# A gated-memory attention layer on TensorE: one head's plain fp32 products regrouped

## What is computed

```python
def chunk_loss(ws, k, lrc, v):
    pred = _mem_mlp(ws, k)                       # silu(k @ w0) @ w1
    return jnp.sum(jnp.mean((pred - v) ** 2, axis=-1) * lrc)
grads = jax.vmap(jax.grad(chunk_loss), ...)(mem_ws, keys, lr, values)   # per chunk of 64 tokens
momentum = _assoc_scan(gm, -grads)
updates = _assoc_scan(gd, momentum)
w0 = mem_w0 + updates[0]
w1 = mem_w1 + updates[1]
x = jnp.einsum('bhncd,bhnde->bhnce', q, w0)
vals = jnp.einsum('bhncd,bhnde->bhnce', jax.nn.silu(x), w1)
vals = _rmsnorm(vals) * (mh_gamma + 1.0) * gate
out = vals @ w_combine
```

## Time and profile before

| | |
|---|---|
| median of three executions | 1114.12 us |
| the profiled execution | 1113.32 us |
| its span, first to last instruction | 1110.8 us |
| granted TensorE clock, mean | 0.987 |
| PE, PEld busy | 96%, 81% of the span |
| DVE, ACT, POOL busy | 62%, 61%, 51% |

### The profile page before, as it was taken

One profiled execution on the slowest core, in us unless ns is written; L12 is line 12 of the kernel. 1 busy time (PEld: TensorE's weight loads), 2 busy tenths in 40 slices (PEclk: granted clock), 3 DMA queues, 4 the chain that ended last, 5 costly groups with the idle time before them and its releaser, 6 DMA issues. The chain is left out here.

```text
span 1110.8 us, 19052 instructions
## 1 busy us (share of the span) xinstructions
PE 1071.7 (96%) x6613; PEld 900.1 (81%) x6613; DVE 686.0 (62%) x1752; ACT 678.7 (61%) x1356; POOL 562.4 (51%) x574
## 2 busy tenths in 40 slices
PE   6899799999999999999999999999999999999994
PEld 4666588888888888888888888888888888888883
DVE  5887566767766555565556555565556555657774
ACT  5776466677655656565556555665566565656663
POOL 6885244478874444344434444444434443444553
PEclk9999699999999999999999999999999999999997
DMA  7210300000030000000000000000000000012221
GB/s 205 79 46 29 105 1 1 1 15 30 21 97 12 19 10 9 8 21 10 9 8 11 20 11 8 9 20 11 8 8 11 20 8 6 6 42 61 69 70 42
DMA packets 42129, 32.66 MB, mean 29 GB/s; under 512 B 4042, under 2 KB 36652, under 8 KB 41900
## 3 DMA queue, kind: packets, MB, share of 16 engines
q1 hardware_dynamic: 38484, 25.93, 8.0%
q0 software_dynamic: 2304, 4.74, 1.3%
q10 hardware_dynamic: 1248, 0.79, 0.2%
HBM read 18.30 MB, written 13.41 MB: 29 GB/s over the span
## 5 line engine op out<-in xcount | busy, mean ns | idle before, releaser
L1040 DVE TENSOR_TENSOR p_sb<-bank,coef 128x512 f32<-128x512 f32 (+3 forms) x512 | 218.8, 483 | 3.1 <-PE bank L749 2.6
L1232 POOL TENSOR_TENSOR sq_rest<-sq,sq_high 128x450 f32<-128x450 f32 x64 | 67.2, 1050 | 245.1 <-ACT sq_high L934 245.1
L772 PE MATMUL bank<-p_sb,err_t 128*128 128x450 f32 (+3 forms) x512 | 132.9, 402 | 0.2 <-DVE p_sb L1040 0.2
L772 PE MATMUL bank<-p_sb,du_t 128*128 128x450 f32 (+3 forms) x512 | 128.8, 394 | 0.0
L772 PEld LDWEIGHTS bank<-p_sb,err_t 128*128 128x128 f32 x512 | 83.7, 190 | 45.5 <-DVE p_sb L1040 25.2
L1236 POOL TENSOR_TENSOR sq_low<-sq_rest,sq_mid 128x450 bf16<-128x450 f32 x64 | 67.6, 1056 | 96.5 <-ACT sq_mid L948 96.2
L772 PEld LDWEIGHTS bank<-p_sb,du_t 128*128 128x128 f32 x512 | 82.1, 190 | 41.4 <-issue 23.9
L1093 DVE SCALAR_TENSOR_TENSOR acc<-bank,rg,acc 128x128 f32<-128x128 f32 x224 | 62.9, 343 | 68.2 <-POOL rg L1220 68.2
L1118 DVE SCALAR_TENSOR_TENSOR du<-q_sb,bank 128x512 f32<-128x512 f32 x64 | 44.0, 688 | 87.7 <-PE bank L749 87.7
L1216 POOL TENSOR_TENSOR rs<-ms,neg_half 128x4 f32<-128x4 f32 x64 | 80.6, 1259 | 28.6 <-DVE ms L1075 27.3
L1207 POOL TENSOR_TENSOR s_low<-s_sb,s_high 128x512 fp32r<-128x512 f32 x64 | 82.7, 1293 | 20.2 <-ACT s_high L911 20.1
(11 more groups left out here) (297 smaller groups left out, 3103.1 us busy)
## 6 DMA issues: line engine op xcount, KB each, us to landing
sorted_rows<-coef SPq DMA_DIRECT2D x5, 516.0 KB, 5.0
rows<-sorted_rows SPq DMA_DIRECT2D x40, 64.5 KB, 1.8
x<-in_L_attn_inputs SPq DMA_DIRECT2D x8, 256.0 KB, 5.5
x_rows<-x SPq DMA_DIRECT2D x8, 256.0 KB, 2.3
ew<-in_L_ffn_w SPq DMA_DIRECT2D x8, 256.0 KB, 3.9
attn_out<-acc SPq DMA_DIRECT2D x7, 256.0 KB, 2.1
ew<-attn_out SPq DMA_DIRECT2D x7, 256.0 KB
ew<-ffn_rows SPq DMA_DIRECT2D x8, 192.0 KB
```

The costliest lines, as they stand in the source:

```text
L772: last = pe.matmul(out[:, P * i:QW], rows[:, i, :], p_sb[:, P_COL[i]:P_COL[i] + QW - P * i], start=False, stop=True, skip_group_check=True)
L1040: last = nc.vector.tensor_tensor(dst, src, w, ALU.mult)
L1232: nc.gpsimd.tensor_tensor(sq_rest[:], sq[:], sq_3[0][:], ALU.subtract).then_inc(g_rest, 1)
```

## The change

On TensorE a step gets a new order. w_x goes right behind the other three projections. The scores are split: `scores_near` (tiles 0 and 1, fp32r) and `scores_far` (tiles 3 and 2, plain). Of s the near ones stay where they were, the far ones go behind VB's product and the block's transpose (which now uses QA), right ahead of the first apply. Of f the far ones go behind the transposes of err (which now use EB), ahead of the error's product; the near ones come behind it. The output rows go ahead of the second apply. The semaphores' counts follow: far tiles count once together, near tiles one by one. VectorE weighs in the new order, and ScalarE copies err_t ahead of the square of vals. The diff, cut to its core:

```diff
-SC_ORDER = [0, 1, 3, 2]
+NEAR, FAR = [0, 1], [3, 2]
@@ TensorE, step
                         project(QA, m.w_qk, f, SHIFT).then_inc(p_qa, 1)
+                        pe.wait_ge(a_xs, n)
+                        project(XB, m.w_x, f, SHIFT)
                     if s is not None:
                         k = n_of(s)
                         pe.wait_ge(v_xl, k + 1)
                         pe.wait_ge(v_p0, SC_BANKS * (k + 1))
-                        scores(s_2[s[1] % 2], xs_2, s_sb[s[1] % 2][:, 2 * P:], xs, p_s1)
-                    if x is not None:
-                        r = s[1] % RING
-                        pe.wait_ge(m.s_rows[r], 16 * (turn(s) + 1))
-                        pe.wait_ge(a_xs, k + 1)
-                        pe.transpose(XB[:, 0:P], m.rows[r][:, 0:D], m.ident[:]).then_inc(p_t, 1)
+                        scores_near(s_2[s[1] % 2], xs_2, p_s1)
                     if f is not None:
                         pe.wait_ge(g_sl, n + 1)
...
                         product(EB[:], [w[:] for w in w1], [part[:] for part in s_2[h % 2]], start=False).then_inc(p_e, 1)
                     if s is not None:
                         pe.wait_ge(v_acc, k)
+                        product(VB[:, 0:QW], [w[:] for w in w1], [part[:] for part in xs_2])
+                    if x is not None:
+                        r = s[1] % RING
+                        pe.wait_ge(m.s_rows[r], 16 * (turn(s) + 1))
+                        pe.wait_ge(a_qa, n + 1)
+                        pe.transpose(QA[:, 0:P], m.rows[r][:, 0:D], m.ident[:]).then_inc(p_t, 1)
+                    if s is not None:
+                        pe.wait_ge(v_p1, SC_BANKS * k + 2)
+                        scores_far(s_sb[s[1] % 2][:, 2 * P:], xs, p_s1)
                         pe.wait_ge(a_et, k + 1)
-                        product(VB[:, 0:QW], [w[:] for w in w1], [part[:] for part in xs_2])
-                        apply(VB, err_t, v_p1, k).then_inc(p_v, 1)
+                        apply(VB, err_t, NEAR)
+                        pe.wait_ge(v_p1, SC_BANKS * k + 3)
+                        apply(VB, err_t, FAR).then_inc(p_v, 1)
...
                     if f is not None:
                         pe.wait_ge(a_err, n + 1)
-                        pe.wait_ge(a_xs, n)
                         for t in range(T):
-                            last = pe.transpose(XB[:, t * P:t * P + P], err[:, t * P:t * P + P], m.ident[:])
+                            last = pe.transpose(EB[:, t * P:t * P + P], err[:, t * P:t * P + P], m.ident[:])
                         last.then_inc(p_et, 1)
+                        pe.wait_ge(a_qa, n + 1)
+                        routing(s)
+                        scores_far(yw, qa, p_s0)
                         pe.wait_ge(v_el, n + 1)
                         pe.wait_ge(v_q, n + 1)
                         product(U[:], [w[:, 3, :] for w in m.w4t], [part[:] for part in err_2]).then_inc(p_d, 1)
                         pe.wait_ge(g_ql, n + 1)
-                        pe.wait_ge(v_p1, SC_BANKS * n)
-                        routing(s)
-                        scores(yk, qa_2, yw, qa, p_s0, SC_ORDER[:-1])
+                        pe.wait_ge(v_p0, SC_BANKS * n + 1)
+                        scores_near(yk, qa_2, p_s0)
                         pe.wait_ge(v_du, n + 1)
+                        pe.wait_ge(a_et, n + 1)
                         for t in range(T):
                             last = pe.transpose(EB[:, t * P:t * P + P], du[:, t * P:t * P + P], m.ident[:])
                         last.then_inc(p_dt, 1)
-                        scores(yk, qa_2, yw, qa, p_s0, SC_ORDER[-1:])
-                        pe.wait_ge(a_et, n + 1)
-                        project(XB, m.w_x, f, SHIFT)
+                    if s is not None:
+                        pe.wait_ge(a_v, k + 1)
+                        for t, r in enumerate(Q_ROWS):
+                            pe.matmul(VB[0:r, t * P:t * P + P], vals[:, t * P:t * P + r], m.w_out[:, s[1], :], start=True, stop=True)
+                    if f is not None:
                         pe.wait_ge(a_dt, n + 1)
-                        apply(XB, du_t, v_p0, n).then_inc(p_x, 1)
+                        pe.wait_ge(v_p0, SC_BANKS * n + 3)
+                        apply(XB, du_t, FAR + NEAR).then_inc(p_x, 1)
                     if x is not None:
                         pe.wait_ge(a_h, x + 1)
...
                     if s is not None:
-                        pe.wait_ge(a_v, k + 1)
-                        for t, r in enumerate(Q_ROWS):
-                            pe.matmul(VB[0:r, t * P:t * P + P], vals[:, t * P:t * P + r], m.w_out[:, s[1], :], start=True, stop=True)
                         pe.wait_ge(g_lo, k + 1)
@@ ScalarE, step: err_t goes ahead of sq and its high part
+                    if f is not None:
+                        act.wait_ge(p_et, n + 1)
+                        nc.scalar.copy(err_t[:].rearrange("p t d -> p (t d)"), EB[:]).then_inc(a_et, 1)
@@ VectorE, step
                         last.then_inc(v_acc, 1)
+                    if s is not None:
+                        dve.wait_ge(p_x, k + 1)
+                        for i in NEAR:
+                            dve.wait_ge(p_s1, SC_BANKS * k + 1 + i)
+                            weigh(s, i).then_inc(v_p1, 1)
                     if x is not None:
...
                     if s is not None:
-                        dve.wait_ge(p_x, k + 1)
-                        weigh(s, p_s1, v_p1, k)
+                        dve.wait_ge(p_s1, SC_BANKS * k + 3)
+                        for i in FAR:
+                            last = weigh(s, i)
+                        last.then_inc(v_p1, 1)
...
                         nc.vector.tensor_tensor(err_2[1][:], err[:], err_2[0][:], ALU.subtract).then_inc(v_el, 1)
-                        dve.wait_ge(v_g, n + 1)
-                        dve.wait_ge(p_d, n + 1)
-                        nc.vector.scalar_tensor_tensor(du[:], q_sb[:], 0.5, U[:], ALU.mult, ALU.mult).then_inc(v_du, 1)
...
-                        weigh(f, p_s0, v_p0, n, s)
+                        dve.wait_ge(p_s0, SC_BANKS * n + 1)
+                        routing_taken(s)
+                        for i in FAR:
+                            last = weigh(f, i)
+                        last.then_inc(v_p0, 1)
+                        dve.wait_ge(v_g, n + 1)
+                        dve.wait_ge(p_d, n + 1)
+                        nc.vector.scalar_tensor_tensor(du[:], q_sb[:], 0.5, U[:], ALU.mult, ALU.mult).then_inc(v_du, 1)
+                        for i in NEAR:
+                            dve.wait_ge(p_s0, SC_BANKS * n + 2 + i)
+                            weigh(f, i).then_inc(v_p0, 1)
```

More of the change, by code:

```diff
@@ L755, in project, with scores_near, scores_far, apply @@
                     return product(out[:, 0:width], [part[:, at[1], :] for part in w], y, stop=stop)
-                def scores(left_2, right_2, left, right, done, tiles=SC_ORDER):
-                    for i in tiles:
-                        out = m.bank[SC_BANK[i]][:, SC_COL[i]:SC_COL[i] + QW - P * i]
-                        if i < 2:
-                            last = product(out, [part[:, i * P:i * P + P] for part in left_2], [part[:, P * i:] for part in right_2])
-                        else:
-                            last = pe.matmul(out, left[:, (i - 2) * P:(i - 1) * P], right[:, P * i:], start=True, stop=True)
-                        if i != 1:
-                            last.then_inc(done, 1)
-                def apply(out, rows, made, n):
-                    for i in SC_ORDER:
-                        if i != 3:
-                            pe.wait_ge(made, SC_BANKS * n + {0: 1, 1: 2, 2: 3}[i])
+                def scores_near(left_2, right_2, done):
+                    for i in NEAR:
+                        out = m.bank[SC_BANK[i]][:, SC_COL[i]:SC_COL[i] + QW - P * i]
+                        product(out, [part[:, i * P:i * P + P] for part in left_2], [part[:, P * i:] for part in right_2]).then_inc(done, 1)
+                def scores_far(left, right, done):
+                    for i in FAR:
+                        out = m.bank[SC_BANK[i]][:, SC_COL[i]:SC_COL[i] + QW - P * i]
+                        last = pe.matmul(out, left[:, (i - 2) * P:(i - 1) * P], right[:, P * i:], start=True, stop=True)
+                    last.then_inc(done, 1)
+                def apply(out, rows, tiles):
+                    for i in tiles:
                         last = pe.matmul(out[:, P * i:QW], rows[:, i, :], p_sb[:, P_COL[i]:P_COL[i] + QW - P * i],
@@ L934, in step @@
                         nc.scalar.copy(sq_3[0][:], sq[:]).then_inc(a_hi, 1)
-                    if f is not None:
-                        act.wait_ge(p_et, n + 1)
-                        nc.scalar.copy(err_t[:].rearrange("p t d -> p (t d)"), XB[:]).then_inc(a_et, 1)
                     if x is not None:
@@ L1028, in places, with weigh @@
                     nc.vector.tensor_tensor(m.per_token[:, 0, :], best, pos, ALU.mult).then_inc(v_alpha, 1)
```

(6 more changed lines are left out.)

24 lines of the change are left out of this document (6 added, 18 removed).

## The result

The change makes the kernel slower: 1185.53 us (median of four, 1185.28 to 1186.56) against 1112.53 us (median of four, 1109.14 to 1114.44) for the kernel before on the same chip, a ratio of 1.066 with an interval of 1.063 to 1.069. That is 73 us, where 1167 and a range of 1140 to 1188 had been forecast: the direction and the main mechanism held, and so did the range, if only by 2.5 us; the loss was undersized by 19 us. The profiled execution took 1185.28 us, its span is 1183.5.

What follows compares the result with a forecast made beforehand. TensorE's instruction stream was taken as the bound; new waits less gains sum to 1.15 us in 40 block heads (46.0) and 0.32 in 24 others (7.7), +53.7 on 1113.3: 1167 us, range 1140 to 1188.

Steps and rivals of the forecast that it cites:

- bias add and register load uncovered: At the next head's start, moved output rows no longer cover this chain: 0.86 us stall in 40 heads, bounds 0.70 and 0.89.
- far weighing ahead of the near scores: Second scores: near ones wait until VectorE has weighed both far tiles; 0.28 us stall in 64 heads, bounds 0.15 and 0.45.
- du_t under the output rows: Before the second apply, 0.89 us of rows cover a 0.96 copy chain; stall 0.06 in 64 heads, bounds 0 and 0.25.
- crossings, w_x: On TensorE, switching between plain fp32 and fp32r costs 0.00 to 0.01 us; fewer crossings and moving w_x counted as 0.
- squares later: ScalarE's square parts come later, but the bf16 sums needing them end the step; put at 0, within du_t's upper bound.
- (e): Sign: w_x weight loads should follow each other at 0.20 to 0.23 us, with nothing gained at their border.
- (a): Sign: the first w_u load should show 0.8 to 0.9 us idle, with the register load right before it.
- (b): Sign: the load for the second set's first near score should wait 0.2 to 0.4 us for p_sb.
- (c): Sign: the load of the second apply should wait for du_t for less than 0.1 us.
- (d): Sign: the waits for p_sb ahead of the first apply should be gone.
- the clock rival: Waits in every head lower TensorE's granted clock; a twentieth of heads at 1.2 GHz adds 40 us: 1205; chance 0.06.
- the one that the tail hides: Register load doesn't wait for the block's bias add, leaving only far-weighing and du_t stalls: 1132 us; chance 0.08.

Runs made afterwards that it cites:

- a_split_wait: The changed kernel with the wait for VectorE's far weighing moved between near tiles 0 and 1 of the second scores; 1160.43 us, ratio 1.043.
- b_xf_later: The kernel before with VectorE's xf of the block moved behind the four weighings of the first apply; 1107.07 us, ratio 0.9946.
- b_extra_in_plain: The kernel before with three extra w_qk products a head among plain products, adding two crossings; 1147.69 us, against 1146.39 for a twin with them among fp32r products.
- experiments 2 to 5: The changed kernel with TensorE's register load ahead of the bias-add wait: 1175.97 us; plus GpSimd's sending later: 1175.2; plus VectorE's weight copy later instead: 1183.45; plus both: 1159.45.
- a_squares_early: The changed kernel with ScalarE's sq and sq_high ahead of err_t and sq_mid ahead of du_t; 1179.28 us, ratio 1.059.
- a_rows_back: The changed kernel with the output rows back behind the block's second product; 1195.27 us, ratio 1.074.
- experiment 8: The kernel before with three extra w_qk products a head, among fp32r products (1146.39 us) or among plain ones with two more crossings (1147.69 us).
- experiments 2 and 4: The changed kernel with TensorE's register load ahead of the bias-add wait (1175.97 us), and the same with VectorE's weight copy behind ms and xs_low (1183.45 us).
- a_load_first: The changed kernel with TensorE's wait for the bias add moved behind the next step's register load; 1175.97 us, ratio 1.057.

## Why the prediction was right, and where its sum was off

| term | forecast, a head | measured | heads |
|---|---|---|---|
| bias add and register load uncovered | 0.86 | 0.87 (0.80 of it as idle time of the w_u load) | 40 |
| far weighing ahead of the near scores | 0.28 | 0.42 with a block, 0.34 and 0.07 at err_low without (a_split_wait) | 64 |
| du_t under the output rows | 0.06 | 0.06 | 64 |
| narrow scores together | 0.05 | 0.05 | 64 |
| near weighing ahead of xf | -0.10 | -0.13 by the loads (b_xf_later alone: -0.14) | 40 |
| less wait at the s_low product | -0.07 | -0.07; +0.26 in the last sequence | 24 |
| crossings, w_x | 0 | 0 to 0.02 | 64 |
| squares later | 0 | 0.8 in a scattering head; in the last sequence 0.85 at s_low and ms, of which the edit returns 0.5 | some 11 |

- *A crossing costs nothing.* Right, and by the reason given: the weight loads, not the starts of the matmul records. The w_x loads of after follow each other at 0.19 and 0.21 (test (e) asked for 0.20 to 0.23), and b_extra_in_plain prices the crossing itself.
- *The main term.* Right to 0.01 us. The chain from the bias add through the register load stood in the earlier trace rows of the kernel before, whose cover the rows were. The sum uses 1.27 for a chain that the prediction's own marks make 1.30 (612.56 to 613.86), the 0.03 between the check's end and the load being taken as slack without saying so; it came out as 1.28. What I had not seen is that it is one of three of similar length; that doesn't change this prediction, only what a repair brings (experiments 2 to 5).
- *Far weighing (mis-sized).* The step took 0.04 us from TensorE's end to VectorE's start, and 0.06 back, from rows of other pairs of instructions. Here they are 0.10 (the far record ends at 604.60, VectorE starts at 604.70) and 0.12 (its end at 605.32, the load at 605.44). Those 0.12 us more are nearly the whole gap of 0.14 in a block head. That err_low may be late in a head without a block and take its part out of this stall was foreseen and came so: 0.07 and 0.34. Over all heads the term is some 8 of the 19 us missed.
- *du_t.* Right: 0.06. Its terms give 0.96 - 0.89 = 0.07, which the sum took as 0.06.
- *The squares (the step that failed).* "the bf16 sums that need them are the last thing in the step, so I put that at 0". I asked only who reads sq_low, and not who queues behind it on the engine that makes it. GpSimd takes the next head's rs, rg and s_low after it, and in some heads a scatter in between. a_squares_early gives back 6 us. The prediction followed SP's queue and not GpSimd's.
- *Output rows as a cover.* Right, and stronger than argued: a_rows_back shows that the same 0.89 us can be spent once. Their new place is a gain in a plain head without a block and makes no difference in one with a block.
- *Tests (a) to (e).* (a) 0.80 with the register load right before it: as asked. (b) asked for 0.2 to 0.4 and shows 0.58 of idle load, of which 0.42 holds up the stream; the upper end was passed either way. (c) 0.06, (d) held. (e) held but for the 0.01. A block head of 16.8 came out 16.97. Its stream without the waits is no shorter than the one of before, so the grouping saved nothing.
- *The range.* The measured time lies 2.5 us inside an upper end that had been drawn 7 us under the sum of the high bounds. Its one bound for late squares (within the 0.25 of du_t) was meant for the sums that read them and not for GpSimd's queue, so it is partly luck that the range held. The price of the clock rival was off too: a twentieth of 64 heads at half speed is some 50 us, not 40.
- *Not settled.* The first head, down by 1.8; and the last head and end, 4.4 us more, where the waits for xs_low, acc and ms grew from 1.5, 0.7 and nothing to 2.4, 1.2 and 0.8. No run takes these apart. The clock rival and the one that the tail hides fell with the window and the load row.

On the pages weighed in the prediction: by the Trainium skill, TensorEngine Tiling (Array Packing), Key Properties, a change of tiling mode drains TensorE. It is about tiling; experiment 8 shows 0 to 0.02 us for a change of precision, so carrying the rule over to it would have been wrong here. By the Trainium skill, DMA: Bandwidth & Descriptors, Latency and other measured facts, a register load takes at least about 600 ns; the trace of after again shows 0.30 for the load's own record, below that figure, and some 0.6 from its start to the next instruction. Where the two differ, the measured rows decide.

## What to carry to other kernels

A piece of work that an engine does at a certain place is also a cover. Before it is moved, list every latency that it hides there, those in the sequencer too, and every chain that starts from the same release: repairing the longest may only bring the next one up. A time for the step from one engine to the other is best taken from the same instructions: here 0.12 us between two such rows was most of the error in one term. For each instruction made later, ask not only who reads its result but who stands behind it in its queue. Where a bank or a buffer is shared by one tile of a group, put the wait at that tile and not ahead of the group; here it was worth 25 us. And add up the groups of weight loads before and after, which shows waits too short for the view of waits: here du_t's 0.06.

## What the runs showed of the hardware that was not expected

- Going between plain fp32 and fp32r products costs nothing measurable (experiment 8: 0 to 0.02 us for two), though on the matmul rows the first interval behind such a border is 0.33 us instead of 0.21. The weight loads are the measure.
- GpSimd's sending with indirect addresses took 1.03 us in one order of VectorE's work beside it and 1.39 us in another (experiments 2 and 4), with nothing changed on GpSimd.
- From a matmul record's end to VectorE's start 0.10 us passed for p_sb behind far scores, against 0.04 for the bias add; from VectorE's end to TensorE's load 0.12 there, against 0.06 behind err_low in a head without a block. One kernel has more than one latency for the same pair of engines.
- A register load holds up the engine's sequencer for some 0.6 us, 0.3 of it the load (L794 above), and it doesn't begin before the wait in front of it is through: 611.3 here, behind the bias add's end at 611.23. In a_load_first, where the wait stands behind it, it begins at 842.4, ahead of the bias add at 843.29.
